# Decoder kernel, layer 0's tile pipeline: the experts two steps behind the top-k search instead of four; layer 1's last three experts loaded on ScalarE's queue

## The reference

```python
# layer 0
x = x + self_attention(ln(x))           # 16 heads of 16
x = x + cross_topk(ln(x), ctx)          # scores over 77 context rows, best 32 of each head kept
x = x + experts0(ln(x))                 # 8 experts of 256x256, top 1, times its probability
# layer 1
x = x + causal_attention(ln(x))
x = x + cross_norm(ctx, ln(x))
x = x + experts1(ln(x))                 # 8 experts, 256 -> 1024 -> 256 with relu, top 1
```

```python
logits = einsum('bsd,ed->bse', x, router_w) + router_b
weights = max(softmax(logits), -1); top1 = argmax(...)
y = take(einsum('bsd,eod->bseo', x, expert_w) + expert_b, top1) * weights
```

## Time and profile before

| | us |
|---|---|
| median of 3 runs | 1976.62 (1974.9 to 1980.56) |
| the profiled execution's own time | 1982.3 |
| its span, first to last instruction | 1980.6 |
| mean granted TensorE clock | 0.879 |
| DVE's first top-k operation | 608.0 |
| last operation of the tile pipeline ends (POOL) | 1116.1 |
| first matmul of layer 1's expert stage (tile turned) | 1740.6 |

### The profile page before, as it was taken

One profiled execution on the slowest core, in us unless ns is written; L12 is line 12 of the kernel. 1 busy time (PEld: TensorE's weight loads), 2 busy tenths in 40 slices (PEclk: granted clock), 3 DMA queues, 4 the chain that ended last, 5 costly groups with the idle time before them and its releaser, 6 DMA issues. The chain is left out here.

```text
span 1980.6 us, 27578 instructions
## 1 busy us (share of the span) xinstructions
PE 1582.6 (80%) x8891; PEld 871.7 (44%) x8892; DVE 1256.1 (63%) x4702; ACT 933.9 (47%) x1831; POOL 518.8 (26%) x427
## 2 busy tenths in 40 slices
PE   4758999999976578888867675999987892369997
PEld 2431222222224366677656442333336672135664
DVE  6988788887507999999980255777735567401111
ACT  2731777777665455555543250666674552111111
POOL 2760000000003354555542142111110433260101
PEclk9965999999897778988878785999999996679999
DMA  6176133331210000000000059236300121781110
GB/s 197 59 202 80 20 45 43 45 43 23 85 44 1 1 1 2 1 1 1 1 1 1 6 157 178 33 55 82 48 1 1 14 39 35 247 202 39 53 41 13
DMA packets 115512, 106.02 MB, mean 54 GB/s; under 512 B 49059, under 2 KB 90091, under 8 KB 115310
## 3 DMA queue, kind: packets, MB, share of 16 engines
q1 hardware_dynamic: 112225, 98.03, 23.5%
q0 software_dynamic: 3152, 6.32, 1.0%
HBM read 71.57 MB, written 36.41 MB: 55 GB/s over the span
## 5 line engine op out<-in xcount | busy, mean ns | idle before, releaser
L1059 DVE TENSOR_REDUCE arena<-banks 128x2 f32<-128x1024 f32 (+1 forms) x448 | 481.0, 1107 | 149.7 <-PE banks L906 94.2
L995 ACT ACTIVATE arena<-banks 128x512 f32<-128x512 f32 (+3 forms) x896 | 439.9, 557 | 187.3 <-PE banks L945 180.6
L906 PE MATMUL banks<-arena 96*128 96x512 bf16 (+3 forms) x896 | 285.9, 396 | 50.0 <-DMA arena<-v 21.1
L945 PE MATMUL banks<-arena 98*128 98x512 bf16 (+3 forms) x896 | 271.9, 364 | 9.1 <-ACT arena L995 6.8
L957 PE MATMUL banks<-arena 128*32 128x512 f32 (+3 forms) x1792 | 220.8, 565 | 12.6 <-ACT arena L995 6.5
L1661 DVE MATCH_REPLACE8 arena<-arena 128x77 f32<-128x77 f32 x1024 | 213.8, 223 | 0.0
L906 PEld LDWEIGHTS banks<-arena 96*128 96x128 bf16 x896 | 80.6, 102 | 233.7 <-DVE arena L1059 136.8
L945 PEld LDWEIGHTS banks<-arena 98*128 98x128 bf16 x896 | 82.3, 98 | 188.0 <-ACT arena L995 124.1
L1556 POOL TENSOR_SCALAR arena<-arena 128x256 f32<-128x256 f32 x32 | 39.1, 1223 | 476.3 <-DVE arena L1642 476.2
L2461 DVE COPY arena<-banks 128x1024 f32<-128x1024 f32 x23 | 28.2, 1224 | 212.3 <-PE banks L2396 212.3
L1657 DVE MAX8 arena<-arena 128x8 f32<-128x77 f32 x1024 | 149.5, 224 | 1.4
(11 more groups left out here) (280 smaller groups left out, 2566.4 us busy)
## 6 DMA issues: line engine op xcount, KB each, us to landing
arena<-parts SPq DMA_DIRECT2D x192, 128.0 KB, 7.5
arena<-in_L_ffn_W SPq DMA_DIRECT2D x16, 1024.0 KB, 13.5
parts<-arena SPq DMA_DIRECT2D x24, 512.0 KB, 9.1
v<-arena SPq DMA_DIRECT2D x32, 256.0 KB, 2.3
arena<-v SPq DMA_DIRECT2D x16, 512.0 KB, 11.1
sorted_rows<-sorted SPq DMA_DIRECT2D x1, 2944.0 KB, 14.2
arena<-sorted SPq DMA_DIRECT2D x23, 128.0 KB, 2.1
arena<-sorted_rows SPq DMA_DIRECT2D x23, 128.0 KB, 2.2
```

The costliest lines, as they stand in the source:

```text
L906: mm = pe.matmul(bank[:, 0:w], qst[r][0:KS, j, i * P:(i + 1) * P], kst[r][0:KS, j, kb * BANK:kb * BANK + w], start=True, stop=not diag)
L945: pe.matmul(bank, kst[r][0:KM, j, kt * P:(kt + 1) * P], qst[r][0:KM, j, half * BANK + lo:(half + 1) * BANK], start=True, stop=True).then_i ...
L995: act.activation(prob[:, gi % 2 * G + j, lo:BANK], PS[:, 4 + n % 3, 0:BANK - lo], ACT.Exp, scale=SCALE).then_inc(sem(s + "_exp"), 1)
L1059: dve.tensor_reduce(m2[u % 2][:, 2 * pair:2 * pair + 2, i, kb], PS[:, 2 * (n % 2):2 * (n % 2) + 2, 0:w], AX.X, ALU.max).then_inc(sem(s + " ...
```

## The change

In `cross_experts` FIRST becomes -2 and LAST - 1 becomes 18. The second half of a tile's way is moved up: the weights, the context, the division and `output` of tile t - 1 all stand in step t, the router, the spread and the first 8 products of tile t - 2 too, and the other 8 products of a tile stand first in the next step. The experts get a bank of their own, `EB` = 1, which is also one of the banks of the scores; the logits move to `OB`. The turning of expert matrices is 3, 3 and 2 a step. On DVE a round is split into `largest` (the 16 `max`) and `taken` (the 16 `match_replace`), and the small work stands between: the router of t - 2 behind round 0, the sums and the division of t - 1 inside round 2, the row statistics inside round 3. POOL normalizes h2 ahead of the difference of the weights. ACT takes one exponential of a constant (`warm`) at the end of steps 0 to 15 and waits for it. In `moe` the loads of experts 5 to 7 leave SP's list; ACT issues them once both DMAs of expert 1 have landed, ahead of its first tile.

```diff
-            PB, WB, QB, OB = 3, 4, 6, 7
-            FIRST, LAST = -3, T + 4
+            EB, PB, WB, QB, OB = 1, 3, 4, 6, 7
+            FIRST, LAST = -2, T + 3
+            TURNS = (3, 3, 2)
...
-                return [w for w, n in ((0, t + 2), (1, t - 3)) if inside(n)]
+                return [w for w, n in ((0, t + 2), (1, t - 1)) if inside(n)]
...
                 for t in range(FIRST, LAST):                      # PE
+                    if inside(t - 3):
+                        experts(t - 3, 1)
+                    if inside(t - 2):
+                        turn_h2(t - 2)
+                        logits(t - 2)
+                    if inside(t + 2):
+                        turn_attended(t + 2)
+                        project(t + 2)
+                    for e in turned(t):
+                        turn_expert(e)
+                    if inside(t - 1):
+                        for c in range(4):
+                            turn_weights(t - 1, c)
+                        context(t - 1)
+                    if inside(t + 1):
+                        turn_h1(t + 1)
+                    if inside(t - 1):
+                        turn_context(t - 1)
                     if inside(t + 1):
                         query(t + 1)
...
+                    if inside(t - 1):
+                        output(t - 1)
                     if inside(t + 1):
                         scores(t + 1)
...
+                        experts(t - 2, 0)
...
                 for t in range(FIRST, LAST):                      # DVE
...
+                    if inside(t):
+                        largest(t, 0)
+                        taken(t, 0)
+                    if inside(t - 2):
+                        router(t - 2)
+                        choose(t - 2)
+                        chosen(t - 2)
+                    if inside(t):
+                        largest(t, 1)
+                        taken(t, 1)
+                    if inside(t):
+                        largest(t, 2)
+                    if inside(t - 1):
+                        sums(t - 1)
+                        normalize(t - 1)
+                    if inside(t):
+                        taken(t, 2)
+                    if inside(t - 2):
+                        gates(t - 2)
+                    if inside(t):
+                        largest(t, 3)
                     if normed(t):
                         row_statistics(t)
...
+                    if inside(t):                                 # ACT, last of its step
+                        act.activation(warm, eps1, ACT.Exp).then_inc(sem(s + "_warm"), 1)
+                        act.wait_ge(sem(s + "_warm"), t + 1)
...
                 for t in range(AHEAD):                            # moe, SP
                     load(t, t % NTB)
-                    if t == NTB - 1:
-                        for e in range(EARLY, E):
-                            load_expert(sp, e)
...
             @block.scalar                                         # moe, ACT
             def _(act):
+                act.wait_ge(sem(f"{s}_w1"), 32)
+                for e in range(EARLY, E):
+                    load_expert(act, e)
```

More of the change, by code:

```diff
@@ L1183, in steps, with turned @@
                 return sum(1 for n in range(FIRST, t + 1) if normed(n))
+            def turned(t):
+                n = t - FIRST
+                return range(sum(TURNS[:n]), sum(TURNS[:n + 1]))
             @block.sync
@@ new lines, in _ @@
+                    if inside(t + 2):
+                        attended(t + 2)
+                        attended_rows(t + 2)
+                    for e in turned(t):
+                        act.wait_ge(sem(s + "_wep"), e + 1)
+                        act.copy(WeT[:, e].rearrange("p k n -> p (k n)"), PS[:, WB + e % 2, :]).then_inc(sem(s + "_weT"), 1)
+                    if inside(t - 1):
+                        for c in range(4):
+                            copy_weights(t - 1, c)
+                        context(t - 1)
@@ new lines, in _ @@
+                    if inside(t + 1):
+                        turned_h1(t + 1)
+                        queries(t + 1)
+                    if inside(t - 2):
+                        router_exp(t - 2)
+                        choice(t - 2)
+                        copy_spread(t - 2, 0)
+                        copy_spread(t - 2, 1)
+                    if inside(t - 1):
+                        mixed(t - 1)
+                    if inside(t - 2):
+                        copy_spread(t - 2, 2)
+                        copy_spread(t - 2, 3)
@@ L1512, in _ @@
+                    if inside(t):
+                        exp_all(t)
+                    if inside(t - 1):
+                        mixed_rows(t - 1)
+                    if inside(t + 1):
+                        copy_scores(t + 1)
                     if normed(t):
                         deviations(t)
[L1514 to L1521 removed]
```

215 lines of the change are left out of this document (68 added, 147 removed).

## The result

| | before | changed |
|---|---|---|
| median of 4 runs, us | 1976.54 | 1924.97 (1924.94 to 1930.65) |
| ratio | | 0.9734 (95%: 0.9717 to 0.9751) |
| profiled execution: time, span | 1982.3, 1980.6 | 1924.96, 1923.2 |
| mean granted clock | 0.879 | 0.911 |
| first top-k search begins | 608.0 | 609.0 |

51.6 us less in the medians where 38 were forecast; by the profiled executions, on which the sum was made, 57.4 against 38. The time is inside the range, near its fast end.

What follows compares the result with a forecast made beforehand. Searches were taken as bound by DVE with PE close behind, the end by a chain through PE, POOL and ACT, layer 1's experts by PE. +2 + 9.4 - 38.6 - 11 = -38 gave 1938.5 us; range 1920 to 1960.

Steps and rivals of the forecast that it cites:

- Part 1: Start of layer 0's pipeline: six turned expert matrices instead of four delay the first search, +2 us (0 to +4).
- Part 2: Layer 0's searches: 14 full steps instead of 12, each at 27.3 us, +9.4 us (-18 from there to +15).
- Rival B: Layer 0's full steps come to DVE's floor, 26.0 us each, 18 us less, 1920 us; chance 0.15.
- three meetings a step: Layer 0's full step: points where moved work and DVE must meet, the argument given against steps at DVE's floor.
- The floor named: DVE's content of a full step in layer 0, 25.9 us together, so 26.0 us as the least step.
- The slack: Layer 0's full step: the new order has one to two microseconds at each meeting, and no more.
- Rival A: `turn_context` and DVE's sums: chain closes on a slow PE, steps near 31 us, +52, 1990 us; chance 0.05.
- Part 3: End of layer 0's pipeline behind the last search: 48.1 us instead of 86.7, -38.6 us (-46 to -31).
- Rival D: End of layer 0's pipeline: its full step without search takes 30 us, not 22, 1947; counted with the forecast's 0.65.
- Part 4: Layer 1's expert weights: fifth tile's wait goes, 12.9 us, first tile 2 us later; -11 us (-13 to -5).
- Rival C: Layer 1: weights delay the scatters as long as they delayed the fifth tile, gain near 0, 1950; chance 0.15.
- the rule of the Trainium skill: Layer 1's weights: all issuing engines' DMAs share 16 engines, so another issuer saves little; sum -27 instead of -38.

Runs made afterwards that it cites:

- b_exp: Kernel before with ACT's long exponential `exp_all` moved behind the copy of the context: 1991.88 us, ratio 0.9987, full steps 27.0 us.
- b_free: Kernel before, experts still four steps behind, with POOL's, ACT's and PE's orders rearranged to clear the step's limits: 1949.31 us, ratio 0.9852.
- a_rt1: Changed kernel with DVE's router, `choose` and `chosen` behind the 16 `max` of round 1, 2.3 us later: 1919.06 us, ratio 0.9716 to the kernel before.
- a_rf: Changed kernel with `router`, `choose` and `chosen` ahead of round 0 again: 2042.38 us, ratio 1.0241 to the kernel before, steps of 33.0 us.
- a_ref: The changed kernel itself, run again in another session: 1947.58 us, ratio 0.9759 to that session's kernel before.
- a_sp: Changed kernel with the loads of experts 5 to 7 back on SP's list: 1954.08 us, ratio 0.9796 to the kernel before.
- a_late: Changed kernel with ACT issuing each pair of expert loads at the head of its first three tiles: 1950.90 us, ratio 0.9781 to the kernel before.
- a_ts: Changed kernel with `choose`'s first instruction as the old `tensor_scalar`: 1927.84 us, ratio 0.9745 to the kernel before.
- a_nowarm: Changed kernel without ACT's `warm` exponential and its wait: 1931.51 us, ratio 0.9753 to the kernel before.

## Why the prediction was right, and where it was off

By the marks of the two profiled executions:

| part | forecast | measured | from |
|---|---|---|---|
| 1, start | +2 | +1.0 | first search 608.04, now 609.05 |
| 2, searches | +9.4 | -6.7 | first search to last `less_max`: 421.3, now 414.6 |
| 3, end | -38.6 | -43.3 | last `less_max` to last addition: 86.7, now 43.4 |
| 4, weights | -11 | -8.7 | +5.0 to the first expert matmul, -13.7 behind it |
| sum | -38 | -57.7 | spans: -57.4 |

**Part 1** was right.

**Part 2 is the step that failed**: "Each I take at 27.3, the measured full step, because PE's work is the same 20.3 us at full clock and DVE still meets PE once per step or more." Rival B's step of 26.0 came instead, and with it the 16 us by which this part is off (the 14 full steps take 26.2 on average, 14 x 1.1). The 27.3 was not a property of the work but of two neighbours: ACT's exponentials ahead of copies that PE needs, and POOL's `less_max` at the moment of DVE's `choose`. The first was seen in the earlier trace rows and then not used; its gain was kept out of the sum, since three meetings a step spoke against it. The second was not seen at all, though the trace of before had it (1.52 us at 704.91): in the step read for the earlier trace rows the wait for PE had covered all but 0.1 us of it (0.31 us at 813.97). b_exp, b_free and a_rt1 show it: 27.0 with only the first gone, 25.6 and 25.7 with both. The floor named, 26.0, was a little too high: the changed kernel's step has 0.3 us of the same wait in it (0.47 for 0.17), and without them it is 25.7.

The slack was told roughly: one to two us at each meeting were named; in the step from 815.23 it is 0.6 us at the logits (they end at 820.33, the router starts at 820.93) and 2.4 at the sums (`turn_context` ends at 828.01, the sums start at 830.40). Rival A, steps of 31 us with PE at 1.2 GHz, is out. a_rf has the router 6 us earlier and pays 7 us a step: there the chain across the step does close, though at the router and not at the sums.

**Part 3** had the right chain. `turn_h2` and the logits put the first router 5.1 us behind the start of `less_max` (forecast 5.7), the full step between the routers takes 20.9 (22.2), the last stretch 17.4 (20.2). Most of the difference is not the change's. From the last `less_max` on the same code takes 43.4 us in the changed kernel's first trace, but 48.3 in that of a_ref and 47.0 in a_sp. Window of the end, a_ref:

```profile
1024.20:1072.50 48.30, 37.08 (x185) 29.64 (x183) 4.84 (x22) 15.08 (x28) 16.50 (x9) 0.79 0.00 1
```

The content is the same 185 records; the clock is 0.79 instead of 0.88, and the 32 context records take 1.93 us there instead of 1.08. The six other traces that have this end (a_ref, a_sp, a_late, a_rt1, a_ts, a_nowarm) take 47.0 to 48.6, so 48.1 was the usual value, and some 4 us of the measured gain are luck of the trace that was profiled first. Whether they are one execution's or its session's, a single trace can't tell; three of that session's four executions took 1924.94 to 1924.97 us. Rival D, an end with a longer step in it, is out.

**Part 4** was right in its mechanism and 2 us too large: the first tile comes 5.0 us later where 2 were taken from a range of 0 to 6.3; a_late shows that it is the weights beside the scatters. The gain behind was 13.7 for 12.9. Rival C, and with it the rule of the Trainium skill that was cited for it, did not hold on this trace: the same engines carry the same bytes, but the fifth tile waited for its turn on SP's list, and that wait goes when the weights leave the list. The rule shows in the 5 us that come back. In the two sessions with the late second tile the part was worth much less, which no row of before could tell.

Of what was to be seen: first search near 610, held; steps of 27.3 and a last search near 1040, missed; the end 48 us, 43.4 in one trace and 47 to 48.6 in the others; the first sorted tile not over 6 us later, held with 5.0.

The gain was thus forecast 16 us too small in part 2 and 5 in part 3, of which 4 are luck, and 2 too large in part 4. The time lies inside the range because the range reached down to rival B's.

What the change is made of, by layer 0's 508.0 us, with the searches (first search to the end of the last) and the end behind them apart:

| | searches | end | layer 0 |
|---|---|---|---|
| before | 421.2 | 86.8 | 508.0 |
| b_free | 403.1 | 76.7 | 479.8 |
| changed | 414.5 | 43.5 | 458.1 |
| a_ts | 417.4 | 48.5 | 465.9 |
| a_rt1 | 408.4 | 47.4 | 455.8 |

Freeing the neighbours without moving the experts gives 28 us (b_free). The two steps fewer on top give 14 to 22: the end is 28 to 33 us shorter than b_free's, but two more of the steps are full ones and a full step is 0.4 longer, so the searches are 11 to 14 longer. The ratios of the last session agree with the lower value: a_ts is 21 us below b_free, and 8.5 of these are part 4's. So, taken in this order, the neighbours are worth more than the shorter pipeline, and a step of 26 us, part 2's 16, does not need the two steps fewer: b_free has it without them. The 0.3 us a step of a_rt1 rest on one trace.

## What to carry to other kernels

Before a steady step is taken as the price of a new order, look at its first steps as well as a middle one, and for each engine at small instructions that last longer than their like: two limits can stand behind each other, and a middle step shows only the outer one. A reordering of neighbours on the helper engines (what stands ahead of the copy that PE waits for, what POOL runs while DVE does small SBUF work) can be worth as much as a shorter pipeline or more, and it is tried first. Leave a list that others wait in order on free of transfers that nobody wants yet, and count what these meet elsewhere.

## What the runs showed of the hardware that was not expected

A DVE instruction of 0.2 us on 8 columns lasted up to 1.85 us; every `tensor_scalar` or `tensor_tensor` of this size that lasted over 0.4 us in the tile pipeline, in all traces of the study, ended within 0.03 us behind the end of a POOL `tensor_tensor`. The kind of DVE instruction made no difference: 0.47 us at the same place in a_ts and in the changed kernel. POOL's 1.22 us `tensor_scalar` (821.74 to 822.97 in the changed kernel) held one that began in its midst, at 822.16, not at all (0.23 us, as in steps where POOL was idle), and others by 0.1 to 0.2 us. The Trainium skill ("SBUF — State Buffer", Who interferes with whom) has a DVE instruction in the fast mode and a GpSimd instruction block each other fully; for POOL's `tensor_scalar` these rows don't show that.

In two of the four sessions ACT and DVE took up the second tile of layer 1's expert stage late, 5 to 6 us behind the end of the last of POOL's 32 scatters of rows and slots, so that the third tile's matmuls came 29 to 36 us behind the second's instead of 9.2. It was on two chips, in kernels with either place of the weights, and on one of these chips gone in the next session. What held them isn't in the trace's releasers and stays open.
